# A gated recurrence with a two-layer network behind it: the second normalised input transposed by DMA instead of TensorE

## The reference

```python
q = layernorm(x); k = v = ctx
r = decay * r + kt * vt                      # elementwise, per step
inp = (qt * r) @ Wi.T + bi
gate = sigmoid(inp @ Wg.T + bg)
state = tanh((gate * state + (1 - gate) * inp) @ A.T + inp @ Bm.T)
x = x + tanh(g_xattn) * (state @ Wo.T + bo)
h = relu(layernorm(x) @ Wq1.T + b1)          # Wq1, Wq2: weights rounded to -1, 0, 1
x = x + tanh(g_ffn) * (h @ Wq2.T + b2)
```

## Time and profile before

| what | value |
|---|---|
| median of 3 runs | 314.29 us (314.02 to 314.38) |
| the profiled execution, its own time | 314.09 us |
| its span, first to last instruction | 312.3 us, so 1.8 us lie around it |
| TensorE clock granted, mean | 0.998 |
| PE busy | 299.2 us (96%) |
| DVE busy | 280.1 us (90%) |
| ACT busy | 238.8 us (76%) |
| POOL busy | 85.3 us (27%) |

### The profile page before, as it was taken

How to read it: one execution, slowest core, us unless ns; L and a number is a source line. 1 busy time by engine, 2 the same in 40 slices (tenths; PEclk the granted TensorE clock), 3 DMA queues, 4 the chain that set the end, 5 groups by cost and what they waited for, 6 DMA issues and landing times. The chain is left out here.

```text
span 312.3 us, 9499 instructions
## 1 busy us (share of the span) xinstructions
PE 299.2 (96%) x3774; PEld 273.4 (88%) x3774; DVE 280.1 (90%) x805; ACT 238.8 (76%) x560; POOL 85.3 (27%) x147
## 2 busy tenths in 40 slices
PE   6989889999999999999999999999999999998995
PEld 4878677899999999999999999999999999996884
DVE  4988999999999999999999999999999998969763
ACT  4688667978878777868878777778788787757693
POOL 3543052131414123132314132132314140141230
PEclk9999999999999999999999999999999999999999
DMA  7933116142514344443514244343424123270321
GB/s 272 392 111 71 68 36 136 37 67 93 101 42 128 51 136 69 136 69 128 78 45 127 36 135 69 136 70 136 67 80 107 33 71 57 71 103 36 67 36 67
DMA packets 19564, 29.45 MB, mean 94 GB/s; under 512 B 1856, under 2 KB 10304, under 8 KB 19392
## 3 DMA queue, kind: packets, MB, share of 16 engines
q0 software_dynamic: 8720, 8.39, 18.9%
q1 hardware_dynamic: 10368, 19.93, 18.3%
q10 hardware_dynamic: 432, 0.53, 0.5%
HBM read 16.26 MB, written 4.19 MB: 66 GB/s over the span
## 5 line engine op out<-in xcount | busy, mean ns | idle before, releaser
L479 ACT ACTIVATE state<-pre_ps,sc 128x64 f32<-128x64 f32 x128 | 40.0, 312 | 45.0 <-PE pre_ps L1079 44.6
L469 ACT ACTIVATE hid<-hid_ps,b_s 128x256 f32<-128x256 f32 x120 | 50.3, 472 | 10.9 <-PE hid_ps L1118 8.9
L1118 PE MATMUL hid_ps<-xt_lo,w_q 128*128 128x256 f16 x240 | 55.5, 272 | 0.0
L1130 PE MATMUL y_ps<-w_q,h_lo 128*128 128x256 bf16 x240 | 55.5, 272 | 0.0
L1118 PE MATMUL hid_ps<-xt_hi,w_q 128*128 128x256 f16 x240 | 55.5, 272 | 0.0
L1130 PE MATMUL y_ps<-w_q,h_hi 128*128 128x256 bf16 x240 | 55.5, 272 | 0.0
L1073 PE MATMUL pre_ps<-m_hi,a_hi 128*128 128x32 f16 x508 | 42.6, 178 | 4.0 <-DVE m_hi L697 3.7
L748 DVE TENSOR_TENSOR h_lo<-hid,h_hi 128x512 f16<-128x512 f32 x60 | 41.3, 688 | 2.4 <-ACT h_hi L475 1.7
L1073 PEld LDWEIGHTS pre_ps<-m_hi,a_hi 128*128 128x128 f16 x508 | 33.5, 96 | 10.3 <-DVE m_hi L697 6.0
L1073 PE MATMUL pre_ps<-m_hi,a_lo 128*128 128x32 f16 x508 | 41.4, 176 | 0.0
L475 ACT CAST h_hi<-hid 128x512 f16<-128x512 f32 x60 | 37.1, 619 | 1.9
(11 more groups left out here) (183 smaller groups left out, 894.1 us busy)
## 6 DMA issues: line engine op xcount, KB each, us to landing
x_norm<-x_in SPq DMA_DIRECT2D x16, 256.0 KB, 2.8
cx<-ctx_in SPq DMA_DIRECT2D x16, 256.0 KB, 3.1
x_res<-x_in SPq DMA_DIRECT2D x16, 256.0 KB, 3.4
x_res<-bo_g POOLq DMA_DIRECT2D x16, 256.0 KB, 4.8
x<-b_g POOLq DMA_DIRECT2D x15, 256.0 KB, 3.8
y_out<-y SPq DMA_DIRECT2D x15, 256.0 KB, 2.0
w_raw<-w_in SPq DMA_DIRECT2D x2, 512.0 KB, 7.1
w_raw<-w_in SPq DMA_DIRECT2D x1, 1024.0 KB, 9.8
```

The lines of the kernel that those rows point to most:

```text
L469: last = nc.scalar.activation(hid[:, p % 2, u, :], hid_ps[p % 2][:, u * N:(u + 1) * N], ACT.Relu, bias=b1_s[:, 2 * p + u:2 * p + u + 1], s ...
L479: nc.scalar.activation(state[:, q[1] % 2, :, step_cols(j)], pre_ps[q[1] % 2][:, :].rearrange("p (k n) -> p k n", k=K)[:, :, step_cols(j)], ...
L1118: last = nc.tensor.matmul(hid_ps[p % 2][:, u * N:(u + 1) * N], w1_q[:, k, cut], v[:, par, k, :], start=n == 0, stop=n == len(terms) - 1)
L1130: last = nc.tensor.matmul(y_ps[:, t * D:(t + 1) * D], h[:, f, t * P:(t + 1) * P], w2_q[:, f, :], start=f == 0 and t == 0 and h is h_hi, st ...
```

## The change

- x_norm is loaded from a second copy of x in which the tokens stand in batch order (b t). `retain` then reads r as it lies; `inp_out` reorders instead, writing inp at a stride of 32 elements.
- `normed_high` and `normed_low` work on xh2 in SBUF, by token, into new tiles xn_hi and xn_lo; SP transposes both by DMA into xt_hi and xt_lo. The four PE transposes of `x1_t` are gone. `normed_high` moves from slot 6 to slot 5, ahead of `gate_out`; `normed_low` from slot 7 to the head of slot 6.
- ACT: `carry` and `square` move from slot 5 to slot 6, with `square` behind `rest_high`; `norm_apply` is split by tile between slots 4 and 7.
- DVE: the scan is cut in two halves, one at the end of slot 6, one in slot 0 of the next pass; `norm_stats` goes behind `state_low`, `norm_mean` into slot 1.
- SP issues the loads a pass earlier and the two transposes last. PE does `y_product` 3 in slot 5 instead of 4. In pass 15 `finish` goes ahead of `hidden_low` 0.

```diff
+            def load_res(q):
+                if exists(plus(q, -2)):
+                    sp.wait_ge(x1_set, upto(plus(q, -2)))
+                sp.dma_start(x_res[:, q[1] % 2, :, :], x_in[number(q)]).then_inc(x_res_in[q[1] % 2], 16)
+
+            def normed_t2(q):
+                if exists(plus(q, -2)):
+                    sp.wait_ge(hid_sum, upto(plus(q, -2), PAIRS))
+                for part, into, made, landed_s in ((xn_hi, xt_hi, xn_hi_set, xt_hi_in), (xn_lo, xt_lo, xn_lo_set, xt_lo_in)):
+                    sp.wait_ge(made, upto(q))
+                    sp.dma_start_transpose(into[:, q[1] % 2, :, :, :].rearrange("p t k n -> p (t k) n"),
+                                           part[:, :, :].rearrange("p t d -> p (t d)")).then_inc(landed_s, 16)
+
             def body(c):
...
+                if exists(plus(c, 3)):
+                    load_norm(plus(c, 3))
+                if exists(plus(c, 1)):
+                    load_res(plus(c, 1))
+                if exists(plus(c, -1)):
+                    normed_t2(plus(c, -1))
...
-                    last = nc.scalar.activation(inp[:, m, :], inp_ps[:, m * N:(m + 1) * N], ACT.Identity,
+                    last = nc.scalar.activation(inp[:, m, :].rearrange("p (t b) -> p b t", t=T),
+                                                inp_ps[:, m * N:(m + 1) * N].rearrange("p (b t) -> p b t", t=T), ACT.Identity,
...
             def normed_high(q):
-                act.wait_ge(xh2_t, upto(q))
-                nc.scalar.mul(xt_hi[:, q[1] % 2, :, :], att_ps[:, :].rearrange("p (k n) -> p k n", k=K), S_X).then_inc(xt_hi_set, 1)
+                act.wait_ge(xh2_set, upto(q))
+                if exists(plus(q, -1)):
+                    act.wait_ge(xt_hi_in, 16 * upto(plus(q, -1)))
+                nc.scalar.mul(xn_hi[:, :, :], xh2[:, :, :], S_X).then_inc(xn_hi_set, 1)
...
+                    if j == 4 and norm:
+                        norm_apply(norm, 0)
                     if j == 5:
+                        if attend:
+                            normed_high(attend)
                         if project:
                             gate_out(project)
+                    if j == 6:
                         if norm:
                             carry(project)
-                            square(norm)
-                    if j == 6:
                         if project:
                             rest_high(project)
-                        if attend:
-                            normed_high(attend)
                         if norm:
-                            norm_apply(norm)
+                            square(norm)
+                    if j == 7 and norm:
+                        norm_apply(norm, 1)
...
                     if j == 6:
+                        if attend:
+                            normed_low(attend)
                         if project:
                             rest_all(project)
-                        if norm:
-                            scan(norm)
+                        if norm and peeled:
+                            scan(norm, (0,))
...
             def hidden_product(q, p):
                 if p == 0:
-                    pe.wait_ge(xt_lo_set, upto(q))
+                    pe.wait_ge(xt_hi_in, 16 * upto(q))
+                    pe.wait_ge(xt_lo_in, 16 * upto(q))
...
-                    if j == 5 and attend:
-                        x1_t(attend)
```

More of the change, by code:

```diff
@@ L119, in build @@
         xh2 = sb("xh2", [P, TILES, D])
-        xt_hi = sb("xt_hi", [P, 2, K, N], f16)
-        xt_lo = sb("xt_lo", [P, 2, K, N], f16)
+        xn_hi, xn_lo = sb("xn_hi", [P, TILES, D], f16), sb("xn_lo", [P, TILES, D], f16)
+        xt_hi = sb("xt_hi", [P, 2, TILES, K, P], f16)
+        xt_lo = sb("xt_lo", [P, 2, TILES, K, P], f16)
         hid = sb("hid", [P, 2, 2, N])
@@ L446, in norm_apply @@
                 act.wait_ge(x_norm_in[q[1] % 2], landed(q))
[L447 to L450, removed]
+                last = nc.scalar.activation(xh1[:, t, :], x_norm[:, q[1] % 2, t, :], ACT.Identity,
+                                            bias=shift1[:, t:t + 1], scale=rs1[:, t:t + 1])
+                if t == TILES - 1:
+                    last.then_inc(xh1_set, 1)
             def state_high(q):
@@ L546, in first @@
                 tanh_step(CHUNK, 0)
-                norm_apply(NEXT_CHUNK)
+                for t in range(TILES):
+                    norm_apply(NEXT_CHUNK, t)
                 tanh_step(CHUNK, 1)
@@ L739, in normed_low @@
             def normed_low(q):
-                dve.wait_ge(xt_hi_set, upto(q))
-                nc.vector.scalar_tensor_tensor(out=xt_lo[:, q[1] % 2, :, :], in0=att_ps[:, :].rearrange("p (k n) -> p k n", k=K),
-                                               scalar=S_X, in1=xt_hi[:, q[1] % 2, :, :],
-                                               op0=ALU.mult, op1=ALU.subtract).then_inc(xt_lo_set, 1)
+                dve.wait_ge(xn_hi_set, upto(q))
+                if exists(plus(q, -1)):
+                    dve.wait_ge(xt_lo_in, 16 * upto(plus(q, -1)))
+                nc.vector.scalar_tensor_tensor(out=xn_lo[:, :, :], in0=xh2[:, :, :], scalar=S_X, in1=xn_hi[:, :, :],
+                                               op0=ALU.mult, op1=ALU.subtract).then_inc(xn_lo_set, 1)
             def hidden_low(q, p):
@@ L916, in body @@
                     if j == 0:
-                        if norm and peeled != 1:
-                            norm_stats(norm)
                         if peeled == 1:
                             scan(project)
+                        elif project:
+                            if peeled > 1:
+                                scan(project, (1,))
                         if attend:
@@ L923, in body @@
                         if norm and peeled != 1:
+                            norm_stats(norm)
+                    if j == 1:
+                        if norm and peeled != 1:
                             norm_mean(norm)
-                    if j == 1:
                         if project:
                             retain(project)
+                        if peeled == NC - 1:
+                            finish(plus(c, -3))
                         if ffn:
                             hidden_low(ffn, 0)
-                        if peeled == NC - 1:
-                            finish(plus(c, -3))
                     if j == 2:
@@ L1255, in body @@
                         y_product(ffn, 2)
-                        y_product(ffn, 3)
                     if j == 4 and project:
```

68 lines of the change are left out of this document (29 added, 39 removed).

## The result

The changed kernel takes 335.69 us (median of 4 runs, 334.56 to 337.66), the kernel before beside it 314.24 (314.02 to 314.38): a ratio of 1.0684, 95% interval 1.0657 to 1.071. The direction was forecast, the size not: 321.5 us with a range of 312 to 332. The profiled execution took 337.66 us with a span of 335.9; before, 314.09 and 312.3.

A forecast was written before the change was run, and what follows sets the result against it. PE's own list was taken as the bound, 17.38 us a pass. 13 x 0.52 = 6.8, -0.3 for `retain`, -0.4 for pass 14, +1.1 at the end: +7.2 on 314.09, 321.3, stated as 321.5 us, range 312 to 332.

The forecast's parts named there:

- m_lo's extra 0.18: Step 7 on PE: with m_hi just in time, m_lo's matmuls start 0.39 after the first, not 0.21, 0.18 more a pass.
- Rival B: Step 7: m_hi's path is short enough, PE stays the bound, the 0.43 is kept 14 times, 308.9 us; 13%.
- What lies beside it: Side costs on DVE and ACT: `retain` 0.75 for 1.08, half scans 0.15 more, strided `inp_out` writes at most 0.14 a pass.
- link 2: ACT after tanh 5: `normed_high` ahead of `gate_out` finds xh2 ready and takes 0.53, so `gate_out` starts at 151.63.
- link 4: DVE: rest starts 0.03 after the gate, takes 0.69, to 153.18; `normed_low` ahead is over by 152.45, costing nothing.
- The links from rest on: Path through rest, rest_hi, `square`, half scan and m_hi to PE's step 7, starting at 155.37, 0.77 late.
- hidden in the loop: Both DMA transposes, 3.4 us each and overlapping, land at 155.9 to 156.5, before `hidden_product` 0 needs xn_lo at 157.68.
- rival C: Transposes land late at `hidden_product` 0 in 14 passes: +12 us, 333, or 51, 373 at 4.8 each; 18%.
- the end: Behind chunk 15 PE stands 1.9 us for the transpose, 0.3 absorbed, `finish` gives back 0.5: net +1.1 us.
- The 0.43 that pass 14 was to keep: Pass 14 has no scan, so it keeps the 0.43 us of the four transposes taken off PE: -0.4 us.

The follow-up runs named there:

- e1: The changed kernel with `square` put ahead of `rest_high` again in ACT's slot 6: 337.37 us (1.0744).
- e5: The changed kernel with the edits of e1 and e2 together, so again without transposing: 311.70 us (0.9912).
- e10: e9 with `inp_out`'s access patterns turned round, writing inp straight and reading its PSUM bank with the stride: 309.69 us (0.9849).
- e12: The changed kernel with one edit, `inp_out` writing inp straight and reading its PSUM bank with the stride: 343.0 us (1.0884).
- e2: The changed kernel without the DMA transposes, xn_hi and xn_lo written in place of xt_hi and xt_lo, data left untransposed: 326.05 us (1.0363).
- e6: The changed kernel with POOL's adding DMAs moved: x_res<-bo_g to the pass's start, x<-b_g until xt_lo has landed, except in the last pass: 329.94 us (1.049).
- e7: The changed kernel with 26 idle matmuls ahead of the last `hidden_product` 0, where PE stands: 334.43 us (1.0645).
- e9: The changed kernel with the edits of e1 and e6, and the last pass's second input transposed on PE as before the change: 313.08 us (0.9955).
- e3: The changed kernel with plain DMA copies of the same bytes in place of the two transposing DMAs, data left untransposed: 329.08 us (1.0458).

## Why the prediction was right in direction and wrong in size

**Right.** That PE's own list stops being the bound and m_hi of step 7 takes its place. PE's wait there was to be some 0.8 us and is 0.79. That this number fits is partly luck: counted from step 5, as the forecast was, step 7 is 1.16 late and not 0.77, and the next paragraph has the rest. DVE's wait for ACT's cx was to be 1.2 us in 13 passes and is 15.9 us in 13; m_lo's extra 0.18 is there (220.76 to 221.15 is 0.39, as in the earlier trace rows); `retain` was to fall to 0.75 and takes 0.67. e1 shows that the half scan's wait is the cause of the late m_hi by taking it away. Rival B, PE still the bound, is what e5 and e10 come near to, once both waits are gone. `finish` in pass 15 was to give back 0.5 and does.

**Wrong, the strided writes of `inp_out`.** The part "What lies beside it" bounded them by 0 and 0.33 us for the two and let at most 0.14 reach a pass, because xh2 was thought 0.2 early in link 2. They cost 0.35 us (1.18 against 0.83), which lies just past the bound taken from the reads the earlier trace rows, and nothing of it is hidden. I had followed it down ACT's list only. It goes down DVE's: inp_lo waits 0.45, x1_apply and `hidden_low` 3 come that much later, normed_high finds xh2 not ready (0.32 behind tanh 5, not 0.21), and `normed_low`, which link 4 had over in time "and costs nothing here", ends 0.2 us after the gate is there: rest starts 2.55 us after step 5, not 2.11. In the forecast's own sum the two ended 0.01 apart (152.45 and 152.46), so `normed_low` had no room. Link 2 was short by itself as well: `normed_high` takes 0.63 to the next start, not 0.53, and 0.61 in e12. The links from rest on are as forecast, and the pass is 18.31, not 17.90: 0.41 in each of 13 passes, 5.3 us. e12 measures the path without the stride at 5.03 us, the forecast at 4.99.

The Trainium skill's rule that the prediction set against this ("SBUF — State Buffer", door 1: lines of 16 bytes, a penalty for each access that falls on a new one) holds for the write, by e10's two rows: 694 against 471 ns. With it the prediction's sum rose by 1.8 us. The stride was worth 0.35 in each of 13 passes, 4.6 us, because the hiding was wrong and not the penalty. The same section of the Trainium skill adds that PSUM has lines of 8 bytes and that a non-contiguous access there slows matmuls; here a strided read of PSUM by ACT costs nothing (471 ns strided in e10, 472 straight before the change), and no run strides a matmul in PSUM.

**Wrong, "hidden in the loop".** The transposes were costed at 3.4 each from the loads, landed by 156.5 in that clock, 1.2 ahead of need. xt_hi did land in 3.4, but xt_lo in 4.9, it can be issued only behind 1.19 us of the first one's issue, and its own takes 1.8 (at times up to 3.3). That made a stand of 0.16 to 1.43 us in seven passes, 5.5 in all: rival C, which had priced it at 12 us or more on top of the forecast, at less than half of its low end. The late step 7 hid the rest. In e1, without it, the stands at `hidden_product` 0 in the loop are 17.7 us; the sum had no term for a wait that the first one covers, and e1, e2 and e5 show that there is one. I had noted that POOL's two DMAs run at that time, and gave it as an argument for rival C, but not as a term; e6, which moves them, has no stand left in the loop.

**Wrong, the end.** 1.9 us of standing were forecast with a landing of 3.4; it was 3.08. xn_lo is made at 309.25, but its transpose is issued at 309.74, behind the 1.49 us that SP needs to issue the first, and it lands 4.0 us later, among x<-b_g. Nothing in the sum stood for the clock behind it: 16 matmuls in 3.57 us and not 1.92, and more until it had recovered. 3.6 us beyond the forecast, net.

The three make 14.4 of the 16.4 us between the forecast for the profiled execution (321.3) and its time. Of the rest 1.1 lies in chunk 0, forecast 0.33 shorter, seen 0.75 longer: 0.35 of it is the strided write again, between steps 4 and 5 (3.14 us, against 2.79 before and in e12), 0.5 lies ahead of step 1, which starts at 20.58 here and at 20.23 in e7 with the same lists up to there, so most of that is spread between executions. The 0.43 that pass 14 was to keep did not come (17.44 us for 17.38): 0.5. The first late passes have the last 0.5. Other runs of the kernel are up to 3.1 us shorter than the profiled one, and it is not shown by what.

The Trainium skill's price that spoke against the change ("VectorE: DVE Perf Modes", the three transpose paths, 1309 ns for a block of 128x128) is not borne out as a sum in series: four blocks land in 2.4 us in e6, with the issue in it, and 0.6 us a block is less than half of it.

## What to carry to other kernels

When work is taken off the bound engine, follow each changed duration down every engine's list to the next thing that the bound engine waits for, and cost waits in series as a stack: the one that is seen covers the next. Before a DMA is put on a path, look at what other queues have in flight in that stretch, and move that first; here that took the second landing from 4.9 to 2.5 us. Try both sides of an instruction for a stride: writing straight and reading PSUM with the stride took 313.08 us to 309.69 once the other waits were gone, and 335.69 to 343.0 while they were there.

## What the runs showed of the hardware

- A transposing DMA of 128x512 f16, SBUF to SBUF, occupies the queue's issue for 1.19 us, a plain copy of the same 128 KB for 0.47. A second one right behind mostly takes 1.27 (up to 2.2), and mostly 1.8 (up to 3.3) while the adding DMAs from POOL are in flight.
- It lands in 2.4 to 2.5 us (medians) away from them (e6, e9, e10), in 3.4 to 5.4 with both of them, in 5.0 and 3.9 with x<-b_g alone (the last pass of e6); x_res<-bo_g in turn takes 5.8 us among the transposes, 4.8 without any (e2), 3.9 moved (e6).
- ACT on 128x256 f32: 471 ns with a read of PSUM at a stride of 32 bytes, 694 ns with a write of SBUF at a stride of 128 bytes. TensorE, fp32r moving operand of 256 columns with a stride of 32 bytes: 418 ns for 301.
- After 3.08 us of standing PE had a granted clock of 0.50 in the next 4.2 us, in the profiled execution, and with idle matmuls in that place (e7) it kept 1.0. It also kept 1.0 after 2.65 us in the profiled execution of e3, and fell to 0.50 for some 3.4 us of e2 (42.6 to 46.0) after a wait of 1.01 us that the kernel before and the changed one have as well, at full clock.
